# A transformer tower on one core: the start and the timetable of the token layers are rebuilt, and the last attention fetches its chosen weights instead of mixing them

## The reference, cut to what matters

```
x = embed[src] + _pos_encoding(s, D)                 # D = 128, 8 heads of 16
for i in range(4):                                   # "token layers"
    q, k, v = heads of x @ Wq[i] + bq[i], x @ Wk[i] + bk[i], x @ Wv[i] + bv[i]
    x = layernorm(x + softmax(q k^T / 4) v @ Wo[i] + bo[i])
    x = layernorm(x + relu(x @ W1[i] + b1[i]) @ W2[i] + b2[i])
h = layernorm(x)
h = h + mixing attention(layernorm(h))
h = h + frequency experts(layernorm(h))
h = h + wide attention(layernorm(h))                 # 8 heads of 128
h = h + chosen attention(layernorm(h)):
    logits = relu(mean over s of x @ r_w1 + r_b1) @ r_w2 + r_b2
    sel = argmax(logits)                             # one of 3 for each sequence
    out = attention of 8 heads of 16 with (wq, wk, wv, wo)[sel]   # 8, 4 or 1 key heads
```

## Time and profile before

| | |
|---|---|
| median of 3 runs | 1198.94 us (1191.29 to 1203.07) |
| profiled execution | 1193.46 us, span of the trace 1191.6 us |
| mean granted clock of TensorE | 0.914 of full speed |
| PE busy | 1010.2 us, 85% of the span |
| DVE, ACT, POOL busy | 649.1, 595.8, 441.4 us |
| token layers | about 33.8 to 541 us of the span |
| chosen attention | woven in from 1049 us, to the end |

### The profile page before, as it was taken

How to read it: one execution, slowest core, us unless ns; L and a number is a source line. 1 busy time by engine, 2 the same in 40 slices (tenths; PEclk the granted TensorE clock), 3 DMA queues, 4 the chain that set the end, 5 groups by cost and what they waited for, 6 DMA issues and landing times. The chain is left out here.

```text
span 1191.6 us, 20631 instructions
## 1 busy us (share of the span) xinstructions
PE 1010.2 (85%) x7098; PEld 714.3 (60%) x7098; DVE 649.1 (54%) x1833; ACT 595.8 (50%) x1332; POOL 441.4 (37%) x633
## 2 busy tenths in 40 slices
PE   0457999999999999843797899997799999976798
PEld 0224655656565565422486587786588888865454
DVE  3255666666666665316456111126277777778874
ACT  3235666666666665514543624425455555532376
POOL 6124656665676665557302000013400000058310
PEclk9778999999999999875698899999799999976799
DMA  4354644544454451002000011010000010005351
GB/s 93 79 117 102 145 101 95 123 93 87 91 129 100 112 105 35 4 1 73 1 1 1 19 27 36 27 32 1 16 12 11 10 38 1 1 1 132 90 126 36
DMA packets 52335, 68.64 MB, mean 58 GB/s; under 512 B 9189, under 2 KB 45057, under 8 KB 48385
## 3 DMA queue, kind: packets, MB, share of 16 engines
q1 hardware_dynamic: 51720, 66.28, 24.1%
q0 software_dynamic: 512, 1.05, 0.6%
HBM read 46.60 MB, written 16.78 MB: 53 GB/s over the span
## 5 line engine op out<-in xcount | busy, mean ns | idle before, releaser
L2212 DVE TENSOR_REDUCE t_nmax<-banks 128x2 f32<-128x512 f32 x256 | 168.0, 685 | 88.9 <-PE banks L2031 87.5
L2147 ACT ACTIVATE t_probs<-banks 128x512 f32<-128x512 f32 x256 | 147.3, 592 | 110.5 <-PE banks L2053 109.7
L2053 PE MATMUL banks<-t_packed 120*128 120x256 bf16 x512 | 100.9, 280 | 27.5 <-DMA t_packed<-t_mT 26.8
L2031 PE MATMUL banks<-t_packed 96*128 96x256 bf16 x512 | 100.1, 278 | 17.5 <-DMA t_packed<-t_qk_pairs 14.5
L2295 POOL TENSOR_SCALAR xhat<-t_rbuf,mv,rstd 128x128 f32<-128x128 f32 x128 | 100.1, 795 | 3.4
L2053 PEld LDWEIGHTS banks<-t_packed 120*128 120x128 bf16 x512 | 42.5, 99 | 82.6 <-issue 38.7
L2031 PEld LDWEIGHTS banks<-t_packed 96*128 96x128 bf16 x512 | 46.3, 99 | 69.3 <-issue 32.5
L2066 PE MATMUL banks<-t_probs,t_v 128*32 128x256 f32 x1024 | 82.5, 395 | 0.0
L853 ACT ACTIVATE hid<-banks,b 128x512 f32<-128x512 f32 x64 | 43.5, 686 | 69.6 <-PE banks L758 68.9
L1186 ACT ACTIVATE l_probs<-banks,l_shift 128x256 f32<-128x256 f32 x128 | 59.4, 471 | 29.8 <-DVE l_shift L1227 27.3
L896 DVE SCALAR_TENSOR_TENSOR acc<-banks,gates,acc 128x128 f32<-128x128 f32 (+1 forms) x72 | 20.1, 342 | 96.8 <-PE banks L778 96.8
(11 more groups left out here) (379 smaller groups left out, 2220.8 us busy)
## 6 DMA issues: line engine op xcount, KB each, us to landing
t_qk_pairs<-t_parts SPq DMA_DIRECT2D x32, 384.0 KB, 2.5
t_packed<-t_qk_pairs SPq DMA_DIRECT2D x32, 384.0 KB, 6.0
t_packed<-t_qk_pairs SPq DMA_DIRECT2D x32, 256.0 KB, 6.8
t_packed<-t_qk_pairs SPq DMA_DIRECT2D x32, 128.0 KB, 7.3
w<-in_L_ffn_w SPq DMA_DIRECT2D x16, 256.0 KB, 2.6
t_packed<-t_mT SPq DMA_DIRECT2D x32, 96.0 KB
...
```

Source lines behind the costliest of these rows:

```text
L2031: ins = pe.matmul(m.mbank[:, n % 3, i * S:(i + 1) * S], m.packed[0:MROW, 0, p, h, c + qt * P:c + (qt + 1) * P], m.packed[0:MROW, 1, p, h, ...
L2053: ins = pe.matmul(scores, m.packed[0:TROW, 1, p, h, c + kt * P:c + (kt + 1) * P], m.packed[0:TROW, 0, p, h, c:c + S], start=True, stop=True)
L2147: act.activation(m.probs[:, n % 6, :], m.sbank[:, n % 2, :], ACT.Exp).then_inc(sem["probs_ready"], 1)
L2212: dve.tensor_reduce(m.nmax[:, b, u // 4, 2 * hp:2 * hp + 2], m.mbank[:, n % 3, :].rearrange("p (i k) -> p i k", i=2), AX.X, ALU.max, negat ...
```

## The change

Three things change.

The start: the setup block has no barrier behind it any more; setup and token layers are one block. POOL gathers the four tiles of pass 0, makes `ident_qk` and orders the weights, and gathers the four tiles of pass 1. The gathers of passes 2 and 3 (GA), the positions (pos, on DVE), the turning (XT on PE) and its copy (XTc on ACT) are now steps of the timetable for passes 0 to 3. RB (POOL adds the output bias to `R`) now waits for XT.

The timetable of the token layers: `PERIOD` is replaced by `STARTS`, 16 starts written out, and all of `PLACES` by new numbers. The same steps run; their order on each engine is another. In steady state PE has AV0.2 and AV0.3 side by side, and AV1.1, AV1.2, AV1.3 too; MT0 stands two M steps earlier. SP has the key loads lk behind x0, not ahead of it, and where a layer changes the order is x0, W, lk, x1. POOL has the steps of the norms in another order.

The last attention: SP writes all three options' weights once to a table in HBM (`option_weights`, 384 rows of 512 floats). rd computes row numbers (`r_index`) instead of `r_hot`. wa and wb are gone; in their place POOL issues two indirect DMAs for each pass (GW, one for each sequence, 128 rows of 2 KB = 256 KB each), and Aq, Ak and V wait for those. `LAST_HEAD` is a new list.

```diff
+    def sync_options(sp):
+
+        rows = r.options.rearrange("(p o) n -> p o n", o=OPTIONS)
+        sp.wait_ge(sem["loaded_ahead"], 16 * len(r.loads))
+        sp.dma_start(rows[:, :, 2 * D:], r.wall[:, :, 2:4, :].rearrange("p o i n -> p o (i n)")).then_inc(sem["g_options"], 16)
+        sp.wait_ge(sem["g_const"], 1)
+        sp.dma_start(rows[:, :, 0:2 * D], r.by_feature[:, :, :, :].rearrange("p o i n -> p o (i n)")).then_inc(sem["g_options"], 16)
 
...
-            pe.wait_ge(sem["g_wqk"], g + 1)
+            pe.wait_ge(sem["g_weights%d" % g], 32)
...
-            for b in range(2):
-                ins = dve.tensor_scalar(r.hot[:, g, b, :], r.key[:, b, :], r.top[:, 1, b:b + 1], None, ALU.is_equal)
-            ins.then_inc(sem["g_hot"], 1)
-            dve.wait_ge(sem["g_hot"], g + 1)
...
-        elif step == "wa":
-            dve.wait_ge(sem["g_hot"], g + 1)
-            for o in range(OPTIONS):
-                for b in range(2):
-                    dst, src = weights(g, b, 0, 2), r.by_feature[:, o].rearrange("p i n -> p (i n)")
-                    if o == 0:
-                        ins = dve.tensor_scalar(dst, src, r.hot[:, g, b, o:o + 1], None, ALU.mult)
-                    else:
-                        ins = dve.scalar_tensor_tensor(out=dst, in0=src, scalar=r.hot[:, g, b, o:o + 1], in1=dst, op0=ALU.mult, op1=ALU.add)
...
-            ins.then_inc(sem["g_wqk"], 1)
+            chain.step(dve.tensor_scalar(r.row[:, :], r.top[:, 1, :], -1.0, r.base[:, 0:1], ALU.mult, ALU.add))
+            dve.tensor_copy(r.index[:, 2 * g:2 * g + 2], r.row[:, :]).then_inc(sem["g_index"], 1)
+            dve.wait_ge(sem["g_index"], g + 1)
...
-        elif step == "wb":
+        elif step == "GW":
             if g == 0:
-                pool.wait_ge(sem["g_const"], 1)
-            pool.wait_ge(sem["g_hot"], g + 1)
-            dst = (m.T if g < 2 else late)[:, 8 * (g % 2):8 * (g % 2) + 8, :].rearrange("p (b i) n -> p b (i n)", b=2)[:, :, 2 * D:]
-            for o in range(OPTIONS):
-                src = r.wall[:, o, 2:4].rearrange("p i n -> p (i n)").unsqueeze(1).broadcast_to([P, 2, 2 * D])
-                ins = pool.tensor_tensor(option if o else dst, src, r.hot[:, g, :, o:o + 1].broadcast_to([P, 2, 2 * D]), ALU.mult)
-                if o:
-                    chain.step(ins)
-                    ins = pool.tensor_tensor(dst, dst, option, ALU.add)
-                if o < OPTIONS - 1:
-                    chain.step(ins)
-            ins.then_inc(sem["g_wvo"], 1)
+                pool.wait_ge(sem["g_options"], 32)
+            pool.wait_ge(sem["g_index"], g + 1)
+            for b in range(2):
+                pool.indirect_dma_start(weights(g, b, 0, 4), None, r.options[:, :],
+                                        bass.IndirectOffsetOnAxis(ap=r.index[:, 2 * g + b:2 * g + b + 1], axis=0)
+                                        ).then_inc(sem["g_weights%d" % g], 16)
...
-PERIOD = 26.16
+STARTS = (0.0, 30.53, 60.92, 91.28, 121.7, 151.97, 182.49, 212.84, 243.18, 273.53, 303.89, 334.38, 364.76, 395.22,
...
-    rows = [(PERIOD * g + at, step, g) for step, at in PLACES[engine] for g in range(LAYER_PAIRS)]
+    rows = [(STARTS[g] + at, step, g) for step, at in PLACES[engine] for g in range(LAYER_PAIRS)]
...
+            if step == "XT":
+                pe.wait_ge(sem["i_sum"], g + 1)
+                bank = use(step, g)
+                for i in range(4):
+                    ins = pe.transpose(bank[:, i * P:(i + 1) * P], m.R[:, 4 * g + i, :], m.ident[:, :])
+                filled(step, g, ins)
...
+            if step == "pos":
+                dve.wait_ge(gathered[g], 64)
+                if g == 0:
+                    dve.wait_ge(sem["i_positions"], 16)
+                for b in range(2):
+                    R = m.R[:, 4 * g + 2 * b:4 * g + 2 * b + 2, :]
+                    ins = dve.tensor_tensor(R, R, m.positions[:, :, :], ALU.add)
+                ins.then_inc(sem["i_sum"], 1)
...
+            if step == "GA":
+                for i in range(4 * g, 4 * g + 4):
+                    pool.indirect_dma_start(m.R[:, i, :], None, t.embed, bass.IndirectOffsetOnAxis(ap=m.ids[:, i:i + 1], axis=0)
+                                            ).then_inc(gathered[g], 16)
+            elif step == "RB":
+                lin_ready(pool, "XT", g)
...
         @block.gpsimd
         def _(pool):
-            pool.wait_ge(sem["q_ready"], 1)
-            for i in range(TILES):
+            pool.wait_ge(sem["i_ids_ready"], 1)
+            for i in range(4):
                 pool.indirect_dma_start(m.R[:, i, :], None, t.embed,
                                         bass.IndirectOffsetOnAxis(ap=ids[:, i:i + 1], axis=0)
                                         ).then_inc(gathered[i // 4], 16)
-            pool.wait_ge(sem["w_proj"], 16)
+            pool.wait_ge(sem["i_ident"], 16)
             pool.tensor_copy(ident_qk[:, :].rearrange("p (d h) -> p d h", h=H), m.ident[:, :].rearrange("p (h d) -> p d h", h=H)
-                             ).then_inc(sem["w_ordered"], 1)
-            pool.wait_ge(sem["w_rest"], 16 * (1 + sum(len(loads) for _, loads in w.loads(t, 0))))
+                             ).then_inc(sem["i_ordered"], 1)
+            pool.wait_ge(sem["i_weights"], 16 * (1 + sum(len(loads) for _, loads in w.loads(t, 0))))
             pool.tensor_scalar(w.by_feature(0, 0), w.by_head(0, 0), DK ** -0.5, None, ALU.mult)
-            pool.tensor_copy(w.by_feature(0, 1), w.by_head(0, 1)).then_inc(sem["w_ordered"], 1)
+            pool.tensor_copy(w.by_feature(0, 1), w.by_head(0, 1)).then_inc(sem["i_ordered"], 1)
+            for i in range(4, 8):
+                pool.indirect_dma_start(m.R[:, i, :], None, t.embed,
+                                        bass.IndirectOffsetOnAxis(ap=ids[:, i:i + 1], axis=0)
+                                        ).then_inc(gathered[i // 4], 16)
```

More of the change, by code:

```diff
@@ L1049, in _ @@
                 sp.dma_start(dst, src).then_inc(sem["loaded_ahead"], 16)
+            chosen.sync_options(sp)
             for step, g in LAST_HEAD["sync"]:
@@ L1351, in route_memory @@
     r.logits, r.key, r.top = sb("r_lg", [P, 2, OPTIONS]), sb("r_key", [P, 2, OPTIONS]), sb("r_top", [P, 2, 2])
-    r.hot, r.share = sb("r_hot", [P, PAIRS, 2, OPTIONS]), sb("r_share", [P, 1])
+    r.base, r.row, r.share = sb("r_base", [P, 1]), sb("r_row", [P, 2]), sb("r_share", [P, 1])
+    r.index = sb("r_index", [P, B], I32)
     r.heads = sb("r_heads", [P, H])
-    r.loads = ((r.w1[:, :], t.all["L1_ffn_r_w1"]), (r.b1[:, :], t.all["L1_ffn_r_b1"].rearrange("(p a) -> p a", a=1)),
+    r.options = nc.dram_tensor("option_weights", [P * OPTIONS, 4 * D], F32)
+    r.loads = ((r.base[:, :], t.all["option_rows"]), (r.w1[:, :], t.all["L1_ffn_r_w1"]), (r.b1[:, :], t.all["L1_ffn_r_b1"].rearrange("(p a) -> p a", a=1)),
                (r.w2[:, :], t.all["L1_ffn_r_w2"]), (r.rows[:, :, :], t.all["route_rows"].broadcast_to([P, 2, OPTIONS])),
@@ L1373, in chosen_attention @@
     recip, otok, oT = sb("recip", [P, 2, 2 * H]), sb("otok", [P, 2, 2, D]), sb("oT", [P, 2, PW])
-    late, term = sb("wsel", [P, TILES, D]), sb("term", [P, 2, 2 * D])
-    option = term[:, :, :]
+    late = sb("wsel", [P, TILES, D])
     stats, mv, vareps, rstd, _ = m.norm_scratch
@@ L1922, in token_layers @@
     slot = {"C1": 0, "C4": 1}
+    gathered = [sem["gathered%d" % g] for g in range(PAIRS)]
     def new_layer(g):
@@ L2338, in tok_transformer @@
     ids, idf = sb("ids", [P, TILES], I32), sb("idf", [P, 2, TILES])
-    pe_sb = sb("positions", [P, 2, D])
+    m.positions, m.ids = sb("positions", [P, 2, D]), ids
     w = m.tok_weights = Names()
@@ L2447, in _ @@
             act.activation(qk_bias[:, :, 1], turned[:, :, 1], ACT.Copy)
-            for g in range(PAIRS):
-                act.wait_ge(sem["lin_ready"][0], g + 1)
-                act.activation(m.xT[:, g * PW:(g + 1) * PW], m.lin[g % 2], ACT.Copy).then_inc(sem["xT_ready"], 1)
-    settle()
-    token_layers(nc, m, t, sem, banks, stack)
+        token_layers(nc, block, m, t, sem, banks, stack)
     settle()
```

800 lines of the change are left out of this document (395 added, 405 removed), and 174 rows, old and new, of tables (LAST_HEAD, PLACES).

## The result

The changed kernel takes 1143.13 us (median of four runs, 1142.86 to 1151.07) against 1198.28 for the kernel before in the same comparison: a ratio of 0.956, 95% interval 0.9497 to 0.9623. The profiled execution has a span of 1141.3 us against 1191.6, so 50.3 us less. The forecast was 1146, with 50 us off the profiled run.

What follows compares the result with a forecast made beforehand. PE was taken to bound the full stretch, chains of waits the start and last attention. Terms −16 −6 −16 +5 −17 = −50 gave 1143.5 from the profiled 1193.46; forecast set at 1146 us, range 1138 to 1154 (0.45).

Steps and rivals of the forecast that it cites:

- Start: From kernel start to Aq of pass 0: Aq at about 17 instead of 33.76 us, −16 us (bounds 12 and 17).
- Fill: Passes 0 and 1: three loads instead of six ahead of x0, 3 us off each, −6 us (0 to −10).
- Steady passes: Twelve passes of the token layers: no wait for x0 and three new AV joins, 1.4 us each, −16 (0 to −22).
- Layer changes: Three places: lk lands late behind SP's wait for weights, 1 to 4.5 us each, +5 in all (0 to +20).
- Drain: End of the token layers and all up to 1049 us: same steps, no new wait, unchanged, ±3 us.
- Last attention: Last attention: DVE loses 27 us of mixing, POOL 23, eight gathers instead; S0.0 at 1100 to 1108; −17 (−2 to −25).
- A: Rival, token layers: period stays, joined AVs wait for exponentials and waits eat both savings; 1162 us, chance 0.20.
- C: Rival, better: lk in time at every layer change, last attention gives 25 or a little more; 1128 us, chance 0.12.
- E: Rival: start bound by weights or ACT's row copies, not gathers; no part but the last moves; 1179 us, chance 0.02.
- B: Rival, last attention: gathers at 3.4 us instead of 1.3 load POOL's queue, gain only 2; 1161 us, chance 0.12.
- D: Rival, every pass: lk behind x0 makes next M0.0 wait; 1206 us at 4 us over, chance 0.04.

## Why the prediction was right, and where its terms were off

The time (1143 against 1146) and four of the six terms came out. That the sum came out within half a us on the profiled run is luck: steady passes and layer changes together gave −4.2, where I had −11, and the other parts gave 7 more than I had.

- Start, −16: −17.2. The margin was as counted; the four gathers ahead of the split cost nothing (each takes 0.94 to 1.07 us to issue, not 1.3). What was not seen is that ACT's row copies end at 15.8 and the turned copy starts at 15.94, so that, as the trace reads, a quicker gather alone would not have helped.
- Fill, −6: −6.4, and S0.0 of pass 0 came 3.2 us sooner after MT0, for which I had 3.
- Steady passes, −16 (0 to −22): −20.8 if the layer changes are held apart. Both savings came: by the run with lk behind x0 in the kernel before, that order is worth 0.95 a pass where I had 0.8 for the wait, and the step from its 26.18 to 25.41, 0.8, is PE's new order, for which I had 0.6 in joins. This term was sized too small, near its own bound.
- Layer changes, +5 (0 to +20): +16. The mechanism was the one named, and so was the landing: I had 14.7 to 18 us after MT0, M0.0 started at 17.1, due at 13.4 (issues 3.3 as counted, the wait 5.8, not 6.7, the loads 7.3 at the long end of 4 to 7). The step that failed is the sum behind it: from 1 to 4.5 a change I took 1.7, though the rows said the middle, about 3; and I charged only the wait, where the clock halves behind it. Measured are 3.2 us of wait and another 2 behind each; nearly all of these 2 are, in the change shown, Aq and Ak at 1.92 each for two matmuls, 1.02 at full clock (the Aq at 271.23 us).
- Drain, 0: −2.4, inside ±3.
- Last attention, −17 (−2 to −25): −20.3, M0.0 and S0.0 where I had them (1086.1 and 1102.8 when counted from the same first tile as before; about 1088 and 1100 to 1108 were named). But the reason was half right. I put it down to DVE and POOL losing 50 us of work. Without the new order that is worth nothing (1168 against 1165): in that trace the late gathers beside SP's transfers hold PE for longer than the mixing did.

One reading was wrong: the first four slices of PE are 0, 4, 5 and 7, so one is empty and not two, and the twelve full ones begin with the fifth; nothing in the sum used it.

The rivals: A did not happen, and the experiment with the AVs apart says why: S waits for exponentials with the AVs apart (3.6 us), not with them joined. C's time, 1128, came only when lk was put ahead of W. E did not happen, though the row copies of ACT that it named are what stands just ahead of the turned copy. B's mechanism, 3.4 us at each gather, is absent: the eight gathers take 0.94 to 1.19 us to issue. A gather's real price is its landing, 2.6 us alone and up to 9.6 beside other transfers, counted from the end of its issue, which B did not have. D, lk too late in every pass, does not occur: lk is due with room to spare outside the layer changes. But the price that D set on such a loop was right in kind: nearly 4 us of wait a pass in the run with lk ahead of x0, there of S for x0, made it 63 us slower.
